# A gated-attention kernel: where VectorE makes the low half of the next tile's normalized rows

## The chip, the cores and the metric

One core of one Trainium2 chip runs the whole kernel. The metric is the device time of one execution in microseconds (us), lower is better; what is compared is the median of several runs. The engines are TensorE (PE in the profile), VectorE (DVE), ScalarE (ACT), GpSimd (POOL) and SyncE (SP, which only issues DMAs here). Each runs its own instruction stream in order; they meet only at semaphores.

## The reference

Two sandwiched blocks work on x of shape (2, 4096, 512) in float32. The first is linear attention over 16 heads, the second a gated linear attention (GLA) with a dense path and four sparse "expert" paths, chosen by a router.

```python
x = x + layernorm(attn(layernorm(x)))
x = x + layernorm(ffn(layernorm(x)))

# attn: q, k = relu(x@Wq), relu(x@Wk);  z = 1/(sum_n(k).q + eps);  out = (v k^T) q * z @ w_proj.T + b
# ffn (xn = layernorm(x)), 8 heads of 64, chunks of 64 rows:
q1, k1, v = xn@Wq*scale, xn@Wk, xn@Wv
q2, k2   = xn@Wqa@Wqb*scale, softmax(xn@Wka@Wkb)
gk1, gk2 = log_sigmoid(xn@Wg1a@Wg1b+bg1)/16, log_sigmoid(xn@Wg2a@Wg2b+bg2)/16
e = softmax(xn@We);  mask = one_hot(argmax(e));  rw = e*mask
o = gla(q1, k1, v, gk1) + sum_e gla(q2*rw_e, k2*rw_e, v, gk2*mask_e)
o = o * rsqrt(mean(o*o)+eps) * norm_w * silu(xn@Wga@Wgb)
return o @ Wo
# gla, chunk by chunk: scores of gated q and k under a causal mask, plus q times the carried state S;
# S <- S*decay + k_out^T v
```

## The kernel before

The rows are cut into 64 tiles of 128 rows (32 for each batch element). A first pass over all tiles normalizes x, makes keys and queries of the attention, writes the queries to DRAM and sums the moments that give the attention's context. The second pass, which takes three quarters of the time, goes over the tiles once more, one **step** for each tile n, and does everything else. A matrix in full precision is kept as a pair of float16 matrices, a high and a low part, and TensorE multiplies with three matmuls (`mm3`: high by high, high by low, low by high). The normalized rows of the second block are such a pair: `xn[:, 0]` and `xn[:, 1]`.

Everything is written out by hand: each engine has its own `step` function, and loops (`Fori`) that hold two steps each. A step is software-pipelined over several tiles. Step n does

- **ahead** for tile n+2: the attention's denominator (`den`), `ahead_qz` and its split into high and low (`ahead_qz_split`), the product with the mixing matrix (`y_mm`), its norm, and the first residual `x1`; ScalarE then makes rstd and the high part of xn (`ahead_norm2`, which increments `xnh_ok`), and VectorE the low part (`ahead_low`, which increments `xn_ok`);
- **front** for tile n: projections, router, gates, gated q and k, scores, state products;
- **back** for tile n-1: carry of the state (`back_carry1`, `back_carry`), masks, the select of the router's expert among the products with the state (`back_select`), the join, and the output's norm;
- **tail** for tile n-2: the output projection and the last residual (`back_out`).

SyncE's queue turns xn of tile n+1 into its transpose xnT with one DMA (`turn_xn`, L238). It waits for `q1_pe`, the last use of the old xnT by TensorE, and then for `xn_ok`. Behind it in the same queue stand the store of an output tile, the loads of two tiles and the transpose of og. TensorE reads the new xnT at the end of step n, in `route(n + 1)` and `low_rank(n + 1)`.

Lines that matter below. On VectorE: L1172 is `ahead_low`; L1198 and L1207 are the carry (the carry waits for `u_pe`, TensorE's state products L470, and for GpSimd's state); L1242 is the first instruction of `front_router`, which waits for the router's matmuls and for `low1_ok`, the third of ScalarE's copies of the low rows (L729 to L731); L1178 and L1186 are the masks of the scores; L1254 and L1257 are `front_onehot`; L1217 and L1220 are the select; L1277 is `front_logsig`; L1161 is the second half of the split of qz; L1314, L1315 and L1321 are the gated products; L1349 is `back_out`; L1168 is the residual x1. On GpSimd: L1044 adds the two masked scores (`back_am`), L1060 multiplies k2 with its gate (`front_k2`); in the first pass L1039 adds keys. On TensorE: L367 is the first matmul of `project_k2`, which waits for the select; L490 the products of q2 with the state, which the select reads; L443 the transposes of gated q and k. On ScalarE: L678 is a square with a row sum, L710 the high part of xn, L716 a residual's copy that waits for `back_out`, L747 the last of three instructions on the gates.

In one step of the state two instructions of the carry are memsets instead of sums: step 32, where the second batch element begins. In the last two steps with a front nothing is done ahead.

Of the kernel before, what the change touches and what calls it, by code (L numbers as in the profile page):

```python
# [10 lines left out]
ALL = BATCH * TILES  # L11
# [35 lines left out]
def sandwich_kernel(nc, x_d, wqkv_d, wproj_d, bproj_d, wb_d, wl_d, ws_d, wo_d, nw_d, consts_d, out_d):  # L47
# [11 lines left out]
    with ExitStack() as ctx:  # L59
# [122 lines left out]
        def S(name):  # L182
            if name not in sems:
                sems[name] = ctx.enter_context(nc.semaphore(name))
            return sems[name]
# [20 lines left out]
        def cur(n):  # L206
            return n + 2

        def prev(n):
            return n + 1  # L210
# [917 lines left out]
        def _(dve):  # L1128
# [29 lines left out]
            def split(n, dst, src, high, done):  # L1158
                ve.tensor_copy(dst[:, 0], src).then_inc(S(high), 1)
                dve.wait_ge(S(high), n + 1)  # L1160
                ve.tensor_tensor(dst[:, 1], src, dst[:, 0], ALU.subtract).then_inc(S(done), 1)  # L1161
# [8 lines left out]
            def ahead_low(n, p):  # L1170
                dve.wait_ge(S("xnh_ok"), cur(n))
                ve.scalar_tensor_tensor(xn[:, 1], x1[:, p, :], rstd[:, 1, :], xn[:, 0], ALU.mult, ALU.subtract).then_inc(S("xn_ok"), 1)  # L1172

            def back_masks(n):
                dve.wait_ge(S("a_pe"), n * 2 + 2)
                dve.wait_ge(S("o_pe"), prev(n))
                for odd in range(2):
                    last = ve.tensor_tensor(am1[:, odd, :, :], bank[(2, 5)[odd]].rearrange("p (a b) -> p a b", a=PAIRS),  # L1178
                                            causal.unsqueeze(1).to_broadcast([P, PAIRS, P]), ALU.mult)
                last.then_inc(S("am1_ok"), 1)  # L1180
# [9 lines left out]
            def back_carry1(n, reset):  # L1190
                dve.wait_ge(S("u_pe"), cur(n))
                dve.wait_ge(S("state_ok"), cur(n))
                if reset:
                    ve.memset(carry0, 0.0).then_inc(S("carry1_ok"), 1)
                    return
                for odd in range(2):
                    h = slice(odd * D2, odd * D2 + D2)
                    last = ve.tensor_tensor(carry0[h, :, h], bank[1][h, 0:PAIRS * D2].rearrange("p (a b) -> p a b", a=PAIRS),  # L1198
                                            state0[h, :, h], ALU.add)
                last.then_inc(S("carry1_ok"), 1)  # L1200

            def back_carry(n, reset):
                if reset:
                    ve.memset(carryx, 0.0).then_inc(S("carry_ok"), 1)
                    return
                for half in range(2):
                    last = ve.tensor_tensor(carryx[:, 2 * half:2 * half + 2, :], bank[3 * half].rearrange("p (r c) -> p r c", r=2),  # L1207
                                            statex[:, 2 * half:2 * half + 2, :], ALU.add)
                last.then_inc(S("carry_ok"), 1)
# [28 lines left out]
            def front_router(n):  # L1238
                dve.wait_ge(S("route_pe"), cur(n))
                dve.wait_ge(S("low1_ok"), cur(n))  # L1240
                logits = bank[7][:, 2 * P:2 * P + NEXP]
                ve.reduce_max(lmax[:, :], logits, X).then_inc(S("lmax_ok"), 1)  # L1242
                dve.wait_ge(S("lmax_ok"), n + 1)
                ve.scalar_tensor_tensor(lscore[:, :], logits, lmax[:, :], score, ALU.is_equal, ALU.mult).then_inc(S("lscore_ok"), 1)
                ve.tensor_scalar(ldiff[:, :], logits, lmax[:, :], None, ALU.subtract).then_inc(S("ldiff_ok"), 1)

            def front_label(n):
                dve.wait_ge(S("lscore_ok"), n + 1)
                ve.reduce_max(lab[:, :], lscore[:, :], X).then_inc(S("lab_ok"), 1)
# [9 lines left out]
            def front_prob(n):  # L1259
                dve.wait_ge(S("lexp_ok"), cur(n))  # L1260
                ve.reciprocal(rr[:, :], lsum[:, :]).then_inc(S("rr_ok"), 1)
                dve.wait_ge(S("rr_ok"), n + 1)
                ve.tensor_scalar(rq[:, :], rr[:, :], D2 ** -0.5, None, ALU.mult).then_inc(S("rq_ok"), 1)
# [72 lines left out]
            def ahead_qz_split(n):  # L1336
                dve.wait_ge(S("qzf_ok"), n + 1)
                dve.wait_ge(S("y_pe"), prev(n))
                split(n, qz16.rearrange("p x a b -> p x (a b)"), qz[:, :], "qzh_ok", "qz_ok")
# [8 lines left out]
                dve.wait_ge(S("x1m_ok"), cur(n))  # L1348
                ve.scalar_tensor_tensor(ob[:, p, :], bank[7], rstd[:, 2, :], xr[:, p, :], ALU.mult, ALU.add).then_inc(S("out_ok"), 1)  # L1349

            def step(n, p, b, front=True, back=True, tail=True, ahead=True, reset=False):
                m, mp, t = n - 1, 1 - p, n - 2
                if back:
                    back_carry1(m, reset)
                    back_carry(m, reset)
                if front:
                    front_router(n)
                    front_label(n)
                if back:
                    back_masks(m)  # L1360
                    back_masks2(m)
                if front:
                    front_masks(n)
                    front_low(n)
                    front_onehot(n, p)
                if back:
                    back_select(m, mp)
                if front:
                    front_prob(n)
                if back:  # L1370
                    back_join(m)
                if front:
                    front_kmax(n)
                    front_kdiff(n)
                    front_logsig(n)
                if back:
                    back_norm(m)
                if front:
                    front_ksum(n)
                    front_lslow(n)  # L1380
                    front_kfac(n)
                    front_sil(n, p, tail)
                if ahead:
                    ahead_qz(n + 2, p, b)
                    ahead_qz_split(n + 2)
                if front:
                    front_gated_1(n)
                    front_gated_q2(n)
                if tail:
                    back_out(t, p)  # L1390
                if front:
                    front_decay(n, p)
                if ahead:
                    ahead_residual(n + 2, p)
                    ahead_low(n + 2, p)

            def tile_stats(g, t):
                u = g * GT + t
# [87 lines left out]
            ahead_low(0, 0)  # L1486
            ahead_residual(1, 1, at=5, again=False)
            ahead_low(1, 1)
            step(0, 0, 0, back=False, tail=False)
            step(1, 1, 0, tail=False)  # L1490
            with dve.Fori(2, TILES - 2, 2) as n:
                step(n, 0, 0)
# [6 lines left out]
                step(n, 0, 1)  # L1499
                step(n + 1, 1, 1)  # L1500
            step(ALL - 2, 0, 1, ahead=False)
            step(ALL - 1, 1, 1, ahead=False)
            step(ALL, 0, 1, front=False, ahead=False)
            step(ALL + 1, 1, 1, front=False, back=False, ahead=False)


def layouts(i):
# [65 lines left out]
```

## Time and profile before

| | |
|---|---|
| median of 3 runs | 2510.76 us (2510.54 to 2510.84) |
| the profiled execution, its time | 2513.41 us |
| its span in the profile | 2511.6 us |
| granted TensorE clock, mean | 0.993 of full |
| TensorE busy | 2401.4 us, 96% |
| VectorE busy | 1782.2 us, 71% |
| ScalarE busy | 1561.9 us, 62% |
| GpSimd busy | 1136.7 us, 45% |

The span is from the first to the last instruction of the profiled execution; "busy" counts an engine's instructions alone. A busy share of 96% says that TensorE has little idle time, and not which wait makes it; that has to be read from a step of the second pass. In a timeline the columns are: start in us, duration in us, engine, line and operation, output and inputs, count, and in square brackets the engine's idle time before it with what ended that. An instruction that is held by something that is no semaphore shows a longer duration, and no idle time. Instructions of one engine overlap by some hundredths, so one may start before the end of the last.

### The profile page before, as it was taken

How to read it: one execution, taken by the hardware profiler on the slowest of the kernel's cores; microseconds unless marked ns; L12 is line 12 of the kernel's file. 1: busy time of each engine (PE TensorE's matmuls, PEld its weight loads, DVE VectorE, ACT ScalarE, POOL GpSimd, SP SyncE). 2: the span in 40 equal slices, each digit the busy share in tenths (PEclk: the TensorE clock that was granted, in tenths of full speed). 3: DMA queues.
4: the chain of work that ended last, by engine and by line, in shares of the span. 5: the costliest groups of instructions: out<-in, count | busy, mean ns of one | idle time of the engine just before them, and what ended most of it. 6: DMA issues, size and time to landing. Idle time of an engine off the chain costs nothing.

```text
span 2511.6 us, 56360 instructions
## 1 busy us (share of the span) xinstructions
PE 2401.4 (96%) x20208; PEld 1431.2 (57%) x20208; DVE 1782.2 (71%) x3484; ACT 1561.9 (62%) x3281; POOL 1136.7 (45%) x929
## 2 busy tenths in 40 slices
PE   4999999997999999999999999999999999999997
PEld 1444444454666666666666666666666666666664
DVE  4444444426778888888777888888887788888875
ACT  2322332226777777777777777777777777777773
POOL 1797333313444444444444444444444444444444
PEclk9999999998999999999999999999999999999998
DMA  6434433311111111111111111111111111111111
GB/s 218 101 100 134 101 101 100 86 53 34 47 44 48 42 46 42 42 42 42 43 48 44 47 44 45 42 42 42 42 46 46 50 42 46 42 42 42 42 26 35
DMA packets 250704, 145.65 MB, mean 58 GB/s; under 512 B 208096, under 2 KB 208096, under 8 KB 250144
## 3 DMA queue, kind: packets, MB, share of 16 engines
q1 hardware_dynamic: 240048, 119.32, 19.1%
q10 hardware_dynamic: 9504, 17.31, 1.8%
q0 software_dynamic: 1104, 8.40, 0.9%
q8 instruction: 28, 0.46, 0.1%
q14 instruction: 20, 0.16, 0.0%
HBM read 61.09 MB, written 33.55 MB: 38 GB/s over the span
## 4 chain that ended last, share of the span: by engine, by line
PE 55%; DVE 24%; ACT 9%; issue 8%; POOL 3%; SPq 1%; DMA 1%; DVEq 0%; ACTq 0%; POOLq 0%
PE psum L319 13%; PE psum L321 13%; PE psum L320 13%; PE psum L586 6%; DVE region L1220 6%; DVE region L1186 3%; ACT junk L678 3%; DVE region L1207 2%; PE psum L331 2%; DVE region L1178 2%; DVE region L1217 2%; ACT region L710 2%; DVE region L1198 2%; ACT region L686 2%; PE psum L367 2%
## 5 line engine op out<-in xcount | busy, mean ns | idle before, releaser
L319 PE MATMUL psum<-wb,region 128*128 128x512 f16 x768 | 293.7, 382 | 0.0
L320 PE MATMUL psum<-wb,region 128*128 128x512 f16 x768 | 292.5, 381 | 0.0
L321 PE MATMUL psum<-wb,region 128*128 128x512 f16 x768 | 292.3, 381 | 0.0
L1056 POOL TENSOR_TENSOR region<-region,kfac 128x512 f32<-128x512 f32 x64 | 66.7, 1042 | 447.2 <-DVE kfac L1309 447.2
L1039 POOL TENSOR_TENSOR region<-region 128x1024 f32<-128x1024 f32 x64 | 147.8, 2309 | 265.9 <-DVE region L1414 233.9
L1414 DVE SCALAR_TENSOR_TENSOR region<-psum,region 128x512 f16<-128x512 f32 x64 | 44.3, 692 | 225.2 <-ACT region L868 225.2
L1044 POOL TENSOR_TENSOR region<-region 128x1024 f32<-128x1024 f32 x64 | 150.9, 2357 | 105.4 <-DVE region L1186 105.4
L1051 POOL TENSOR_SCALAR region<-region,m 128x512 f32<-128x512 f32 x256 | 172.6, 694 | 26.8 <-DVE hm L1257 26.8
L586 PE MATMUL psum<-region 128*128 128x512 f16 x768 | 176.2, 379 | 2.1 <-DVE region L1414 2.1
L1084 POOL TENSOR_TENSOR og<-og 128x512 f16<-128x512 f32 x64 | 74.2, 1160 | 190.8 <-ACT og L810 190.8
L1172 DVE SCALAR_TENSOR_TENSOR region<-region,rstd 128x512 f16<-128x512 f32 x64 | 48.1, 752 | 143.2 <-ACT region L710 143.2
L1220 DVE SCALAR_TENSOR_TENSOR region<-psum,m,region 128x512 f32<-128x512 f32 x192 | 144.2, 751 | 6.8
L1168 DVE SCALAR_TENSOR_TENSOR region<-psum,rstd,region 128x512 f32<-128x512 f32 x64 | 48.1, 751 | 140.8 <-issue 138.1
L686 ACT ACTIVATE region<-psum 128x512 f32<-128x512 f32 x256 | 137.3, 589 | 0.0
L1410 DVE TENSOR_TENSOR region<-region 128x512 f16<-128x512 f32 x64 | 102.4, 1600 | 49.0 <-ACT region L881 49.0
L763 ACT ACTIVATE region<-psum 128x512 f32<-128x512 f32 x64 | 38.2, 597 | 156.9 <-PE psum L321 156.9
L1067 POOL TENSOR_TENSOR region<-region,decay 128x512 f32<-128x512 f32 x64 | 67.0, 1047 | 150.9 <-DVE decay L1326 150.9
L1060 POOL TENSOR_TENSOR region<-region 128x512 f32<-128x512 f32 x64 | 81.3, 1271 | 111.2 <-ACT region L777 111.2
L453 PE MATMUL psum<-region 64*128 64x128 f32 x2048 | 131.5, 278 | 0.0
L490 PE MATMUL psum<-region 64*128 64x256 f32 x1024 | 129.5, 393 | 2.0 <-DVE region L1178 2.0
L319 PE MATMUL psum<-wqk,region 128*128 128x512 f16 x256 | 97.7, 382 | 34.3 <-DMA region<-region 34.3
L586 PEld LDWEIGHTS psum<-region 128*128 128x128 f16 x768 | 74.9, 98 | 93.5 <-DVE region L1414 3.6
(232 smaller groups left out, 7252.4 us busy)
## 6 DMA issues: line engine op xcount, KB each, us to landing
region<-x_in SPq DMA_DIRECT2D x128, 256.0 KB, 2.6
q_cols<-region ACTq DMA_DIRECT2D x64, 256.0 KB, 2.5
region<-q_cols SPq DMA_DIRECT2D x64, 256.0 KB, 2.8
out_rows<-region SPq DMA_DIRECT2D x62, 256.0 KB, 2.0
region<-wb_in POOLq DMA_DIRECT2D x1, 3072.0 KB, 11.5
region<-wqkv_in SPq DMA_DIRECT2D x4, 512.0 KB, 6.1
region<-region SPq DMA_TRANSPOSE x128, 3.0
region<-ws_in POOLq DMA_DIRECT2D x1, 1280.0 KB, 15.6
```

Of the source, the lines that this page charges most:

```text
L319: mm(out, lhs(0), rhs(0), start=start, stop=False)
L320: mm(out, lhs(0), rhs(1), start=False, stop=False)
L321: return mm(out, lhs(1), rhs(0), start=False, stop=stop)
L453: last = mm(bank[where[odd]][:, pr * P:(pr + 1) * P], kT[h, pr, :], qT[h, pr, :], start=True, stop=True)
L490: last = mm(psum[:, 2 * half + odd, r * 256:r * 256 + 256], q2T[h, 2 * half + r, :], statex[h, 2 * half + r, :], start=True, stop=True)
L586: last = mm(bank[4 + j], xn8[:, p * GT + t, x * C + j * P:x * C + (j + 1) * P], k16[:, y_, :], start=first and begins, stop=final and ends ...
L686: ac(dst.rearrange("p a b -> p (a b)"), bank[where], ACT.Copy).then_inc(S(done), 1)
L1039: nc.gpsimd.tensor_tensor(kacc[b], kacc[b], k16, ALU.add).then_inc(S("kacc_ok"), 1)
L1044: nc.gpsimd.tensor_tensor(am1[:, :, :, :], am1[:, :, :, :], am2[:, :, :, :], ALU.add).then_inc(S("am_ok"), 1)
L1051: last = nc.gpsimd.tensor_scalar(vm[:, e, :], v[:, p, :], m4[:, p, e:e + 1], 1.0, ALU.mult, ALU.mult)
L1220: ve.scalar_tensor_tensor(to, of[:, :, e, :], m4[:, p, e:e + 1], to, ALU.mult, ALU.add).then_inc(S("sel_ok"), 1)
L1410: ve.tensor_tensor(xn8[:, p * GT + t, C:2 * C], xf, xn8[:, p * GT + t, 0:C], ALU.subtract).then_inc(S("xn8_ok"), 1)
```

## The change

In a step of the second pass, VectorE called `ahead_low(n + 2, p)` as its very last action. It now calls `ahead_low(n + 1, mp)` in the middle of the step, between `ahead_qz_split` and `front_gated_1`. A tile's low rows are thus made one step later than before. The prologue still makes those of tiles 0 and 1; step 0 makes none, steps 1 to 62 make those of tiles 2 to 63. Nothing else moves on any engine, and no instruction is added or taken away.

```diff
-            def step(n, p, b, front=True, back=True, tail=True, ahead=True, reset=False):
+            def step(n, p, b, front=True, back=True, tail=True, ahead=True, reset=False, late=True):
...
                 if ahead:
                     ahead_qz(n + 2, p, b)
                     ahead_qz_split(n + 2)
+                if late:
+                    ahead_low(n + 1, mp)
                 if front:
                     front_gated_1(n)
                     front_gated_q2(n)
...
                     front_decay(n, p)
                 if ahead:
                     ahead_residual(n + 2, p)
-                    ahead_low(n + 2, p)
...
-            step(0, 0, 0, back=False, tail=False)
+            step(0, 0, 0, back=False, tail=False, late=False)
...
             step(ALL - 2, 0, 1, ahead=False)
-            step(ALL - 1, 1, 1, ahead=False)
-            step(ALL, 0, 1, front=False, ahead=False)
-            step(ALL + 1, 1, 1, front=False, back=False, ahead=False)
+            step(ALL - 1, 1, 1, ahead=False, late=False)
+            step(ALL, 0, 1, front=False, ahead=False, late=False)
+            step(ALL + 1, 1, 1, front=False, back=False, ahead=False, late=False)
```

VectorE's instructions at the turn of a step in the loop, before (in brackets what each waits for; `xnh_ok` is ScalarE's high part of xn, `u_pe` TensorE's state products, `low1_ok` ScalarE's low rows):

```order
L1326 TENSOR_TENSOR decay<-exs 128x20 [waits state_ok,exs_ok]
L1168 SCALAR_TENSOR_TENSOR region<-psum,rstd,region 128x512 [waits xc_ok,rstd0,x1m_ok]
L1172 SCALAR_TENSOR_TENSOR region<-region,rstd 128x512 [waits xnh_ok]
L1198 TENSOR_TENSOR region<-psum,region 64x4x64 [waits state_ok,u_pe]
L1198 TENSOR_TENSOR region<-psum,region 64x4x64
L1207 TENSOR_TENSOR region<-psum,region 128x512 x2
L1242 TENSOR_REDUCE lmax<-psum 128x1 [waits low1_ok,route_pe]
```

In the changed kernel the residual L1168 and the carry L1198 are neighbours there; the rest is as it was. The middle of the step on VectorE, after the change (`qzh_ok` is VectorE's own high part of qz, `q1_pe` TensorE's projection of q1):

```order
L1159 CAST region<-region 128x512 [waits y_pe,qzf_ok]
L1161 TENSOR_TENSOR region<-region 128x512 [waits qzh_ok]
L1172 SCALAR_TENSOR_TENSOR region<-region,rstd 128x512 [waits xnh_ok]
L1314 SCALAR_TENSOR_TENSOR region<-psum,region 128x512 [waits q1_pe,e1_ok]
L1315 SCALAR_TENSOR_TENSOR region<-psum,region 128x512
```

Before, L1314 stood right behind L1161; now L1172 is between them, with no other semaphore than its own. The streams of TensorE, ScalarE, GpSimd and SyncE are the same in both kernels.

## Rows read from the trace of the kernel before

**Rows 1.** Windows from L367 to L367: length; busy PE, PEld, DVE, ACT, POOL; clock, DMA.

```profile
1154.14:1184.03 29.89, 29.20 (x279) 18.52 (x279) 23.99 (x50) 21.92 (x47) 13.71 (x12) 1.00 0.17 44
1482.66:1512.43 29.77, 29.20 (x278) 18.52 (x279) 23.90 (x50) 21.90 (x47) 13.72 (x12) 1.00 0.17 45
1512.43:1542.02 29.59, 29.20 (x278) 18.52 (x279) 23.37 (x48) 21.72 (x47) 13.69 (x12) 1.00 0.20 45
```

**Rows 2.** Waits of TensorE, 1000 to 2300 us: total, times, longest.

```profile
PE psum L367 <- DVE region L1220: 29.3, 44, 0.7
```

**Rows 3.** Timeline of all engines, turn of a step in the loop.

```profile
1170.10 1.90 PE L470 MATMUL psum<-region 128*64 128x256 f32 x16
...
1171.52 0.72 ACT L710 ACTIVATE region<-region,rstd 128x512 f16<-128x512 f32 x1
...
1172.28 0.75 DVE L1172 SCALAR_TENSOR_TENSOR region<-region,rstd 128x512 f16<-128x512 f32 x1 [2.25 <-ACT region L710]
...
1172.95 0.85 DVE L1198 TENSOR_TENSOR region<-psum,region 64x256 f32<-64x256 f32 x2
...
1173.78 0.38 ACT L729 ACTIVATE region<-psum 64x256 f16<-64x256 f32 x1 [0.57 <-PE psum L321]
...
1174.44 0.26 ACT L731 ACTIVATE region<-psum 64x128 f16<-64x128 f32 x1
```

**Rows 4.** Timeline of all engines, router to one-hot rows of the same step.

```profile
1175.04 0.15 DVE L1242 TENSOR_REDUCE lmax<-psum 128x1 f32<-128x4 f32 x1
...
1176.88 1.28 DVE L1186 TENSOR_TENSOR region<-psum,same_c 128x512 f32<-128x512 f32 x2
...
1178.24 2.36 POOL L1044 TENSOR_TENSOR region<-region 128x1024 f32<-128x1024 f32 x1 [1.58 <-DVE region L1186]
...
1178.41 2.00 PE L490 MATMUL psum<-region 64*128 64x256 f32 x16
...
1180.06 0.56 DVE L1254 TENSOR_SCALAR m<-cst,lab 128x4 f32<-128x4 f32 x1
```

**Rows 5.** Timeline, the same step behind the select.

```profile
1184.46 1.49 ACT L747 ACTIVATE region<-region 128x1536 f32<-128x1536 f32 x1
...
1186.10 1.75 DVE L1277 SCALAR_TENSOR_TENSOR region<-psum,region 128x1536 f32<-128x1536 f32 x1
```

**Rows 6.** Timeline, last step with a front; none moved ahead of it.

```profile
2456.09 0.26 ACT L731 ACTIVATE region<-psum 64x128 f16<-64x128 f32 x1
...
2456.45 0.16 DVE L1242 TENSOR_REDUCE lmax<-psum 128x1 f32<-128x4 f32 x1 [0.28 <-ACT region L731]
...
2458.19 1.28 DVE L1186 TENSOR_TENSOR region<-psum,same_c 128x512 f32<-128x512 f32 x2
```

**Rows 7.** Timeline of all engines, split of qz to the next norm, loop step.

```profile
1192.69 0.69 DVE L1161 TENSOR_TENSOR region<-region 128x512 f16<-128x512 f32 x1
...
1193.45 1.26 POOL L1060 TENSOR_TENSOR region<-region 128x512 f32<-128x512 f32 x1 [1.75 <-ACT region L777]
...
1194.27 0.69 DVE L1314 SCALAR_TENSOR_TENSOR region<-psum,region 128x512 f32<-128x512 f32 x1 [0.89 <-PE psum L321]
1194.36 1.23 SPq L238 DMA_TRANSPOSE region<-region  x1
...
1196.91 0.72 ACT L716 ACTIVATE region<-region,xkeep 128x512 f32<-128x512 f32 x1 [1.70 <-DVE region L1349]
...
1197.63 1.91 PE L443 MATMUL psum<-cst,region 128*128 128x128 f32 x16
1197.83 0.60 ACT L678 ACTIVATE junk<-psum 128x512 f32<-128x512 f32 x1 [0.20 <-PE psum L321]
```

**Rows 8.** Landing times of L238's DMAs, whole kernel.

```profile
DMA to landing us min/median/max: 3.0/3.0/4.8
```

**Rows 9.** Timeline, first pass, VectorE and GpSimd side by side.

```profile
400.74 2.36 POOL L1039 TENSOR_TENSOR region<-region 128x1024 f32<-128x1024 f32 x1 [5.41 <-DVE region L1414]
...
401.88 1.77 DVE L1410 TENSOR_TENSOR region<-region 128x512 f16<-128x512 f32 x1 [0.77 <-ACT region L881]
```

## The prediction, made before the changed kernel ran

> **What bounds the kernel now.** I read the second pass, since the change touches nothing else. Cutting it at the starts of one TensorE instruction, the first matmul of `project_k2` (L367), gives one step per window [rows 1]. A step inside VectorE's loops lasts 29.89 us and TensorE is busy for 29.20 of it, so 0.69 us is all that a better order can win from a step. TensorE's waits name that remainder: L367 waits 29.3 us in 44 steps, 0.67 each, for VectorE's L1220, the last product of the select [rows 2]. So TensorE runs through from L367 to the end of `intra` and then stands until the select is done.
>
> Now follow VectorE back from L1220. At the turn of a step [rows 3] it waits until 1172.28 for ScalarE's L710, runs L1172 (`ahead_low`, 0.75), and starts the carry, L1198, at 1172.95. TensorE's L470, which the carry really needs, had ended at 1172.00. Behind the carry comes the router's L1242 at 1175.04, although ScalarE's L731, which it needs, ended at 1174.70: 0.34 late. From L1242 on VectorE is back to back until L1186 ends at 1178.16 [rows 4]. GpSimd's L1044 (`back_am`) starts 0.08 later and runs until 1180.60; the little L1254 (`front_onehot`) starts at 1180.06 but ends at 1180.62, right behind L1044. Its 0.56 us for four columns is a wait for GpSimd. Hot rows, select and L367 follow. So the chain per step is L1172, carry, router, masks, GpSimd's add, one-hot, select, L367, and the delay of 0.34 us passes through it whole.
>
> **The change, part by part.**
>
> *Taken from the turn of the step:* the wait for L710 and L1172 itself, which costs 0.67 us in line (1172.28 to 1172.95 [rows 3]). The carry may then start with `u_pe`. In the last step with a front, where the step ahead of it has no `ahead_low`, the same carry runs and the router starts at 2456.45, 0.10 behind L731's end, after 0.28 of idling [rows 6]. This is what the changed kernel should look like in every step. The floor is L731 (TensorE's low-rank products, then ScalarE), which the change does not move. So L1242 gains 0.34 - 0.10 = 0.24 us, and not 0.67.
>
> *How much of it arrives.* From L731's end to L1186's end it is 3.46 in the loop [rows 3, 4] and 3.12 in that last step [rows 6]; 0.10 of the difference is that L1242 to the end of L1186 takes 3.12 in the loop and 3.02 in the last step, which I leave aside: 0.24 again. A second sample in the trace: in the step that resets the state, the carry is two memsets (it comes between 1512.43 and 1542.02), and this step took 29.59 against 29.77 of its neighbour [rows 1]. TensorE's busy time is the same, 29.20. The gain was 0.18. I take 0.22 for a loop step, with 0.18 and 0.24 as bounds.
>
> *What could bind next on this chain.* L1254 must start before GpSimd is through. It starts 0.54 before GpSimd's end, so an add that ends 0.24 earlier still ends last. The select needs TensorE's L490, which ends at 1180.41, while L1254 ends at 1180.62 and the hot rows follow [rows 4]: 0.21 of room plus the hot rows, about enough.
>
> *Put in between the split of qz and the gated products:* 0.67 us where VectorE idles 0.89 before L1314, waiting for TensorE [rows 7]. That shrinks a little. L1277 (`front_logsig`) needs ScalarE's L747, which ended 0.15 before it [rows 5]; ScalarE hangs on TensorE's gates, ahead of L367, and does not move with the gain. With a latency of 0.04 (L710 to L1172 [rows 3]) only 0.11 of the gain passes L1277, so relative to L367 everything behind it on VectorE comes 0.11 later, and the idle time is 0.78. 0.67 fits, with 0.11 to spare, and costs nothing. If that cover were gone, ScalarE has 0.20 before L678 (the norm of the tile ahead) and 0.57 before L729 (the low rows): nothing is late on the chain before these are used up [rows 3, 7]. The last tile's `xnh_ok` that the moved instruction waits for is a step old: no wait.
>
> *What waits for it later:* SyncE's transpose L238 waits for `q1_pe`, and then for `xn_ok`, which used to be a step old. It was issued at 1194.36 [rows 7]; the new `xn_ok` comes at about 1192.69 + 0.11 + 0.61 + 0.75 = 1194.16. Behind it in SyncE's queue stand the store, the two loads and og's transpose. It lands in 3.0 us, 4.8 at most [rows 8], and the router's matmuls read it behind L470, one step after 1172.00, so at 1201.8: 7.4 us after the issue. Even a microsecond of delay is covered.
>
> *Sum.* VectorE's loops hold 56 steps; the first still belongs to the pipeline's filling. 55 x 0.22 = 12.1. Six steps more (two of the filling, three around the middle, the last but one) I take at 0.13, my choice between nothing and the reset step's 0.18 since the filling waits for other things: 0.8. The reset step and the last have their gain already. Together 12.9 us. The profiled execution took 2513.41 us with a span of 2511.6 and would come to 2500.5; the median of the runs, 2510.76, which is 2.65 below, to 2497.9.
>
> **Rivals.**
>
> *The shared access of VectorE and GpSimd.* In the first pass L1410, a tensor_tensor with both inputs in SBUF, takes 1.77 us where it starts beside GpSimd's L1039 and ends at 403.65, 0.55 behind L1039's end of 403.10 [rows 9]; L1161, of the same shape, takes 0.69 [rows 7]. So it stood until GpSimd was nearly through. L1172 too reads two SBUF tensors, and its new place is beside GpSimd's L1060 (k2 times its gate). Counted from L367's start at 1184.03, L1060 starts at 9.42. L1172 would start at 8.66 (L1161) + 0.11 + 0.61 = 9.38 (the next instruction starts 0.08 before the end of one of this size, as L1198 behind L1172), first by 0.04, with an uncertainty as large. If VectorE is first, L1060 is held until about 10.0 and its product comes at 11.3, while TensorE's transposes (L443) only start at 13.6 [rows 7]: free. If GpSimd is first, L1172 ends 0.61 behind L1060's end (10.68), at 11.29, and L1314 starts at 11.21 for 10.24, 0.97 late. L1349 hands this to L716; L716 then starts at 13.85, L678 at 14.48 for 13.80, 0.68 late. The 0.57 before L729 take most, and 0.11 reaches the low rows. The gain would be 0.11 in such a step: 55 x 0.11 + 0.8 = 6.9, so 2503.9; if it alternates from step to step (a smaller gain puts L1172 earlier again), 10 us and 2501. This rival I give 0.20.
>
> By the Trainium skill ("SBUF — State Buffer", Who interferes with whom) a VectorE instruction with two SBUF inputs and a GpSimd instruction that reads SBUF exclude each other, and the order of issue decides who stands. By that rule the move is not free in either order; the trace agrees for tensor_tensor with the 1.77 us of L1410, and shows no long overlap for the form that is moved.
>
> *Nothing is won.* Another wait takes the 0.22: the select finds L490 (0.21 of room) or the one-hot finds its rows, or TensorE's cumulate finds VectorE's low logs later by the 0.11. Against it stands the reset step, which kept 0.18 with all of these in place. A gain under 0.09 a step is within 5 us: 2506 to 2511. Chance 0.07.
>
> *Slower.* It needs one thing: L1172 stuck in its new place for longer than all covers. 0.97 late still leaves 0.11 won, so the break-even is L1314 late by 1.08, and 5 us are lost from 1.17 on; each 0.1 beyond costs 5.5 us. GpSimd's L1060 would have to hold it for 0.2 longer than its own 1.26 us allow, or start later than it does, and ScalarE's L777, on which L1060 waits, moves with TensorE. At 1.3 late: 2523. Chance 0.03.
>
> **The numbers.** Forecast (VectorE first, or the delay swallowed), 0.70: its own range is 55 x 0.18 + 0.5 = 10.4 to 55 x 0.24 + 1.0 = 14.2, so 2496.5 to 2500.4. Lock collision 0.20, nothing 0.07, slower 0.03. The range must leave out no more than 0.2: from 2495.5, a little under the upper bound of the gain, to 2505, past the collision in every step. A measurement of this kernel tells 0.2%, 5.0 us, from no change. Forecast and nearly all of the collision are beyond it: faster 0.90, same 0.07, slower 0.03.
>
> **What the profile after would show.** L1242 idles before it, released by L731, and starts 0.10 behind it; L1198 starts well under 0.95 behind L470's end; TensorE's wait before L367 falls from 0.67 to about 0.45; the step lasts 29.65 in the loops; L1172 has no wait; the idle time before L1314 is near 0.1. L1060 starting as before but lasting about 1.8 says VectorE was first; L1172 at nearly 2 us and L1314 a microsecond late says GpSimd was. I am wrong if the step keeps its 29.88 (then look at what L1254 or L1217 ends its wait on), or if ScalarE's L729 is no longer released by TensorE.

## The result, and the profile after

The changed kernel takes 2498.91 us (median of 5 runs, 2496.37 to 2500.06) against 2510.84 (5 runs, 2510.54 to 2512.97): a ratio of 0.9947, 95% interval 0.9936 to 0.9958 (the ratio is the one that belongs to the interval; the two medians divide to 0.9952). It is faster by 11.9 us between the medians, half a per cent; 2497.9 was forecast.

| | before | after |
|---|---|---|
| the profiled execution, its time | 2513.41 us | 2496.37 us |
| its span | 2511.6 us | 2494.6 us |
| granted TensorE clock, mean | 0.993 | 0.995 |
| first to last L1242 (63 steps) | 1881.36 us | 1867.98 us |
| a step in the loops, mean of 55 | 29.875 us | 29.645 us |

The profiled execution of after was the fastest of its five, so the spans differ by 17.0 us, more than the medians do. Of this the second pass made 13.4. The pass began 2.55 us earlier (first L1242 at 572.54 instead of 575.09) though nothing ahead of it was changed; the granted clock was 0.97 there between 500 and 560 us instead of 0.94. Another 1.1 us lies behind the last L1242. What the change is worth is best read from the pass.

The windows from L367 to L367 answer to [rows 1]; columns as there.

```profile
1117.49:1147.13 29.64, 29.20 (x278) 18.48 (x279) 25.15 (x50) 21.75 (x47) 13.68 (x12) 1.00 0.17 44
1147.13:1176.78 29.65, 29.20 (x278) 18.43 (x278) 25.15 (x50) 21.78 (x47) 13.70 (x12) 1.00 0.17 44
```

TensorE's busy time is unchanged, VectorE's is 1.16 more for the same 50 instructions: one of them has become longer, as is shown below. TensorE's wait in the same stretch as [rows 2]:

```profile
PE psum L367 <- DVE region L1220: 19.3, 43, 0.7
```

That is 0.45 us each time instead of 0.67. The turn of the step and the select, which answer to [rows 3, 4]:

```profile
1133.46 1.90 PE L470 MATMUL psum<-region 128*64 128x256 f32 x16
...
1135.41 0.86 DVE L1198 TENSOR_TENSOR region<-psum,region 64x256 f32<-64x256 f32 x2 [1.42 <-PE psum L470]
...
1137.80 0.26 ACT L731 ACTIVATE region<-psum 64x128 f16<-64x128 f32 x1
...
1138.16 0.16 DVE L1242 TENSOR_REDUCE lmax<-psum 128x1 f32<-128x4 f32 x1 [0.58 <-ACT region L731]
...
1141.36 2.35 POOL L1044 TENSOR_TENSOR region<-region 128x1024 f32<-128x1024 f32 x1 [1.34 <-DVE region L1186]
...
1141.78 2.00 PE L490 MATMUL psum<-region 64*128 64x256 f32 x16
...
1143.24 0.50 DVE L1254 TENSOR_SCALAR m<-cst,lab 128x4 f32<-128x4 f32 x1
...
1143.96 0.75 DVE L1217 TENSOR_SCALAR region<-psum,m 128x512 f32<-128x512 f32 x1
...
1147.13 0.39 PE L367 MATMUL psum<-ws,region 128*128 128x512 f16 x1 [0.43 <-DVE region L1220]
```

The carry starts 0.05 behind L470's end (0.95 before), and the router's L1242 stands idle and starts 0.10 behind L731's end (0.34 before). The middle of the next step, answering to [rows 7]:

```profile
1155.94 0.69 DVE L1161 TENSOR_TENSOR region<-region 128x512 f16<-128x512 f32 x1
...
1156.55 1.82 DVE L1172 SCALAR_TENSOR_TENSOR region<-region,rstd 128x512 f16<-128x512 f32 x1
1156.56 1.26 POOL L1060 TENSOR_TENSOR region<-region 128x512 f32<-128x512 f32 x1 [1.61 <-ACT region L777]
...
1158.30 0.68 DVE L1314 SCALAR_TENSOR_TENSOR region<-psum,region 128x512 f32<-128x512 f32 x1
...
1160.92 0.72 ACT L716 ACTIVATE region<-region,xkeep 128x512 f32<-128x512 f32 x1 [2.60 <-DVE region L1349]
...
1161.55 0.58 ACT L678 ACTIVATE junk<-psum 128x512 f32<-128x512 f32 x1
```

There is most of the 1.16: L1172 now lasts 1.82 where it took 0.75, with no idle time ahead of it, and ends beyond GpSimd's L1060, which starts 0.01 after it and keeps its 1.26. It stood until L1060 was nearly through. (The rest is overlap of neighbours, which busy time counts once: the durations by themselves add up to 1.03 more.) This is so for 56 of the 64 L1172; the durations of the two lines (ns, least, median, most) say it:

```profile
L1172 DVE SCALAR_TENSOR_TENSOR region<-region,rstd x64: 744/1832/1851, 565.2 to 2429.2; 128x512 f16<-128x512 f32 x64
L1060 POOL TENSOR_TENSOR region<-region x64: 1262/1269/1840, 589.7 to 2458.8; 128x512 f32<-128x512 f32 x64
```

What hangs on L1172 is late at first: L1314 starts 11.17 behind L367, L716 13.79 and L678 14.42, where it was 10.24, 12.88 and 13.80. ScalarE no longer idles before L678 and, in most steps, before L729; and L729 starts 0.107 behind the start of TensorE's L453 in both kernels (means over the loops). So L1172 became 1.07 us longer in the middle of the step, and of the 0.62 that were left of it at L678 nothing passed ScalarE's 0.57 us of idle time before L729. The little that is missing is overlap: where ScalarE does not idle, an instruction starts up to 0.1 before the recorded end of the last.

### The profile page after: what moved, and what is told of

It is laid out like the page before. It is cut to its first block and busy times, and to the rows that moved or that the text cites. A ratio compares the mean times of both kernels' runs of the same rounds, so it can differ in the third digit from the quotient of the medians.

```text
span 2494.6 us, 56360 instructions
## 1 busy us (share of the span) xinstructions
PE 2397.7 (96%) x20208; PEld 1424.4 (57%) x20208; DVE 1848.0 (74%) x3484; ACT 1554.0 (62%) x3281; POOL 1138.6 (46%) x929
## 5 line engine op out<-in xcount | busy, mean ns | idle before, releaser
L1039 POOL TENSOR_TENSOR region<-region 128x1024 f32<-128x1024 f32 x64 | 147.8, 2309 | 266.2 <-DVE region L1415 233.7
L1044 POOL TENSOR_TENSOR region<-region 128x1024 f32<-128x1024 f32 x64 | 150.5, 2352 | 92.3 <-DVE region L1186 92.3
L1067 POOL TENSOR_TENSOR region<-region,decay 128x512 f32<-128x512 f32 x64 | 67.1, 1048 | 199.0 <-DVE decay L1326 199.0
L716 ACT ACTIVATE region<-region,xkeep 128x512 f32<-128x512 f32 x64 | 46.3, 723 | 156.3 <-DVE region L1349 156.3
L1168 DVE SCALAR_TENSOR_TENSOR region<-psum,rstd,region 128x512 f32<-128x512 f32 x64 | 48.1, 751 | 123.4 <-issue 120.7
L1084 POOL TENSOR_TENSOR og<-og 128x512 f16<-128x512 f32 x64 | 74.1, 1158 | 139.7 <-ACT og L810 139.7
L453 PE MATMUL psum<-region 64*128 64x128 f32 x2048 | 131.5, 278 | 0.0
L1060 POOL TENSOR_TENSOR region<-region 128x512 f32<-128x512 f32 x64 | 83.7, 1307 | 104.0 <-ACT region L777 104.0
L490 PE MATMUL psum<-region 64*128 64x256 f32 x1024 | 127.9, 389 | 2.0 <-DVE region L1178 2.0
```

Source lines behind the costliest of these rows:

```text
L453: last = mm(bank[where[odd]][:, pr * P:(pr + 1) * P], kT[h, pr, :], qT[h, pr, :], start=True, stop=True)
L490: last = mm(psum[:, 2 * half + odd, r * 256:r * 256 + 256], q2T[h, 2 * half + r, :], statex[h, 2 * half + r, :], start=True, stop=True)
L1039: nc.gpsimd.tensor_tensor(kacc[b], kacc[b], k16, ALU.add).then_inc(S("kacc_ok"), 1)
L1044: nc.gpsimd.tensor_tensor(am1[:, :, :, :], am1[:, :, :, :], am2[:, :, :, :], ALU.add).then_inc(S("am_ok"), 1)
```

## Experiments

All kernels are edits of the changed kernel (called "after") unless it is said otherwise. The ratio is to runs of the kernel before that were taken beside them (medians 2510.65 to 2512.71). "Step" is the mean of the same 55 steps in VectorE's loops.

| run | edit | median us | ratio to before, 95% | step us |
|---|---|---|---|---|
| (after) | | 2498.91 | 0.9947, 0.9936 to 0.9958 | 29.645 |
| e1_behind_carry | L1172 behind the carry | 2499.16 | 0.9945, 0.9929 to 0.9962 | 29.650 |
| e9_ahead_of_split | L1172 ahead of the split | 2498.23 | 0.9946, 0.9929 to 0.9963 | 29.642 |
| e2_behind_gated | L1172 behind the gated products | 2497.44 | 0.9942, 0.9925 to 0.9959 | 29.644 |
| e2b_behind_decay | L1172 behind front_decay | 2502.77 | 0.9963, 0.9949 to 0.9977 | 29.644 |
| e3_twice | L1172 twice | 2525.20 | 1.0052, 1.0035 to 1.0068 | 30.02 |
| e4_after_onehot | one-hot ahead of the masks | 2551.95 | 1.0165, 1.0148 to 1.0182 | 30.50 |
| e8_gated_onehot | e2 and e4 | 2554.27 | 1.0170, 1.0153 to 1.0187 | 30.57 |
| e6_before_onehot | kernel before, one-hot as e4 | 2557.74 | 1.0185, 1.0168 to 1.0202 | 30.59 |
| e10_between_masks | one-hot between the masks | 2498.56 | 0.9946, 0.9930 to 0.9963 | 29.633 |
| e11_mask_alone | half of the one-hot there | 2497.33 | 0.9941, 0.9925 to 0.9958 | 29.630 |
| e12_select_halves | e10, select in halves | 2498.55 | 0.9948, 0.9935 to 0.9962 | 29.65 |
| e13_halves_alone | select in halves | 2507.61 | 0.9982, 0.9973 to 0.9991 | 29.79 |

### Where did the gain come from: L1172 behind the carry

```diff
                     back_carry(m, reset)
+                if late:
+                    ahead_low(n + 1, mp)
                 if front:
                     front_router(n)
...
-                if late:
-                    ahead_low(n + 1, mp)
```

> VectorE makes the low rows of tile n+1 at the turn of step n, but behind the carry and ahead of the router. The same work stands ahead of the router as in the kernel before; only its wait for ScalarE no longer stands ahead of the carry. Theory A (the router's floor is ScalarE's third copy of the low rows, and the wait ahead of the carry was what mattered): the carry starts right behind TensorE's L470, the 0.57 us that VectorE idles before the router in the changed kernel take the 0.67 us of the moved instruction, the router starts at most 0.1 later behind ScalarE's copy than in the changed kernel; a loop step of 29.65 to 29.75 us, 2499 to 2505 us. Theory B (the 0.67 us of work ahead of the router was what mattered): the router stays about 0.3 behind the copy, a step of 29.85 us, 2509 to 2511 us. No collision with GpSimd's L1060 in either; VectorE's L1314 is released by TensorE again.

```profile
1167.99 0.86 DVE L1198 TENSOR_TENSOR region<-psum,region 64x256 f32<-64x256 f32 x2 [2.01 <-PE psum L470]
...
1170.09 0.74 DVE L1172 SCALAR_TENSOR_TENSOR region<-region,rstd 128x512 f16<-128x512 f32 x1
...
1170.39 0.26 ACT L731 ACTIVATE region<-psum 64x128 f16<-64x128 f32 x1
...
1170.75 0.16 DVE L1242 TENSOR_REDUCE lmax<-psum 128x1 f32<-128x4 f32 x1
```

The step is 29.650, as short as the changed kernel's, with L1172 still between the carry's start and the router. Its 0.74 fill the idle time for L731, and L1242 starts as early behind L731 as in after, 0.10. So theory A held. The numbers add up: in the kernel before, the carry stood 0.90 later than it had to behind L470 (0.95 instead of 0.05), 0.67 of it L1172's work and 0.23 the wait for L710 [rows 3]. VectorE's 0.58 of idle time before L1242 and the 0.08 by which neighbours overlap cover the work. What cost 0.23 a step was thus the wait that came on top. The work by itself is free here because this cover is as long as the work, and not in general.

### Does the collision cost: three other places

```diff
 e9:            ahead_qz(n + 2, p, b)
+               ahead_low(n + 1, mp)
                ahead_qz_split(n + 2)
 e2:            front_gated_q2(n)
+               ahead_low(n + 1, mp)
                back_out(t, p)
 e2b:           front_decay(n, p)
+               ahead_low(n + 1, mp)
                ahead_residual(n + 2, p)
```

> The changed kernel with the moved instruction one place earlier, between ahead_qz and its split. Theory A (order of issue decides who stands; now the split's L1161 meets L1060 and TensorE's y_mm waits for it): L1161 is held until L1060 is nearly over, 1.8 us, qz comes about 0.5 us later than TensorE wants it, step up to 30.1 us, 2510 to 2526 us, or less if VectorE wins the race in every other step. Rival (the place among VectorE's instructions is of no account, since 0.1 to 0.8 us are idle there): 29.65 us, 2497 to 2500 us.

> The moved instruction stands behind the three gated products and ahead of back_out, where GpSimd's L1060 is over. Theory A (the collision of the changed kernel is swallowed by ScalarE's idle time and costs nothing): the instruction takes 0.75 us again instead of 1.83, L1314 starts 10.2 us behind L367 instead of 11.2, and the step stays at 29.65 us, 2497 to 2500 us. Rival (the collision reaches the low rows by up to 0.11 us a step): the step falls to 29.55 to 29.6 us, 2493 to 2496 us.

> The moved instruction stands behind front_decay and ahead of the residual, where VectorE waits some 2 us anyway: it uses no cover at all, but SyncE's transpose can only be issued some 14.2 us behind L367, 3.4 us before TensorE's router matmuls want its result. Theory A: with a landing time of 3.0 us nobody waits, step 29.65 us, 2497 to 2500 us. Rival (the late transpose becomes the wait): TensorE idles before the router's matmuls, each 0.1 us of it lengthens a step by 0.1; at the 4.8 us of the slowest landing seen a step of 31 us and 2580 us.

In e2 no L1172 of the 64 lasts over 0.752 us: there is no collision, and the step is 29.644 against 29.645. The collision costs nothing, as theory A had it. In e9 it is L1161, a tensor_tensor with two SBUF inputs, that meets GpSimd, first by 0.08:

```profile
1217.06 0.69 DVE L1161 TENSOR_TENSOR region<-region 128x512 f16<-128x512 f32 x1
1217.14 1.74 POOL L1060 TENSOR_TENSOR region<-region 128x512 f32<-128x512 f32 x1 [1.61 <-ACT region L777]
1217.96 0.69 DVE L1314 SCALAR_TENSOR_TENSOR region<-psum,region 128x512 f32<-128x512 f32 x1 [0.21 <-PE psum L321]
```

VectorE wins, GpSimd lasts 1.74, and L1314 has 0.21 of idle time again. Theory A, by which that place costs up to 0.45 a step, fell: 29.642, the rival's value. In e2b the loops are as fast, but the last step with a front takes 28.60 instead of 27.45 and one in the middle 30.17 instead of 29.63. (In e2 they are 27.86 and 29.74, and after has 27.45 and 29.63.) The median, 2502.77, lies beyond the 2497 to 2500 of theory A, which holds for the loops alone; these two steps add 1.7 us to after's time. The transpose of xn, which waits for L1172, is too late for TensorE in a step that is shorter than the others:

```profile
2437.48 0.75 DVE L1172 SCALAR_TENSOR_TENSOR region<-region,rstd 128x512 f16<-128x512 f32 x1
...
2438.31 1.23 SPq L238 DMA_TRANSPOSE region<-region  x1
...
2441.40 0.18 PE L319 MATMUL psum<-wl,region 128*128 128x4 f16 x1 [1.09 <-DMA region<-region]
```

The place is not free of a meeting with GpSimd either: L1172 starts 0.16 ahead of L1067 (the state's decay), keeps its 0.75, and L1067 takes 1.49 (median) instead of 1.05. The loops show no cost of it.

### How much can VectorE carry there: L1172 twice

```diff
+        spare = sb("spare", 2, C, dt=f16)
...
             def ahead_low(n, p):
                 dve.wait_ge(S("xnh_ok"), cur(n))
+                ve.scalar_tensor_tensor(spare[:, p, :], x1[:, p, :], rstd[:, 1, :], xn[:, 0], ALU.mult, ALU.subtract)
```

The kernel does the work once more into a tensor that nobody reads.

> The changed kernel with the moved instruction issued twice in its new place, the first time into a spare tensor. Theory A (the delay of 1 us by the collision has used up ScalarE's idle time before its low rows exactly, so any further delay reaches the router): L729 comes 0.4 to 0.65 us later, the step is 30.05 to 30.3 us, 2523 to 2538 us. Rival (there is more cover left than ScalarE's idle time shows): 29.65 to 29.75 us, 2497 to 2505 us.

```profile
1198.40 0.75 DVE L1173 SCALAR_TENSOR_TENSOR spare<-region,rstd 128x512 f16<-128x512 f32 x1
1198.55 1.73 POOL L1061 TENSOR_TENSOR region<-region 128x512 f32<-128x512 f32 x1 [1.75 <-ACT region L778]
1199.07 1.76 DVE L1174 SCALAR_TENSOR_TENSOR region<-region,rstd 128x512 f16<-128x512 f32 x1
```

The line numbers are one or two higher here. The first takes the access and GpSimd is held, then the second is held by GpSimd. Counted from L490, the second ends about 0.62 later than L1172 does in after. The step grows by 0.375 us (30.02, just under theory A's least of 30.05), so some 0.25 of cover were left in after. The way is not only the expected one over ScalarE's low rows. Before L367 TensorE waits 0.58 a step instead of 0.45; and the second half of its state products (L470, here L471), which waits for the residual L1168 (here L1169), is held by it, as it never is in after: its weight loads stand for 0.47 us. By TensorE's starts in three steps, some 0.15 of the delay stand at L367 and 0.2 at L470.

```profile
1205.33 0.75 DVE L1169 SCALAR_TENSOR_TENSOR region<-psum,rstd,region 128x512 f32<-128x512 f32 x1 [1.89 <-issue]
...
1206.13 0.63 PEld L471 LDWEIGHTS psum<-region 128*64 128x64 f32 x8 [0.47 <-DVE region L1169]
```

### Is L1254's wait for GpSimd the next thing to win: the one-hot ahead of the masks

```diff
                     front_label(n)
+                    front_onehot(n, p)
                 if back:
                     back_masks(m)
...
                     front_low(n)
-                    front_onehot(n, p)
```

> The changed kernel, with the one-hot rows (L1254, L1257) made right behind the router's label instead of behind the low rows, so that GpSimd's add L1044 cannot hold them. Theory A (L1254's 0.50 us is GpSimd's hold, and the next floor is TensorE's L490): L1254 takes 0.2 us or less, the select starts 0.1 to 0.15 behind L490's end, which is 0.04 to 0.08 earlier than now; step 29.56 to 29.61 us, 2493 to 2497 us. Rival (L1254 is long for a reason of its own, 0.5 us wherever it stands): the masks come 0.5 later, the step is 29.65 us or longer, 2499 us or more.

> Both orders together: the moved instruction behind the gated products (no collision with L1060) and the one-hot rows behind the label. Theory A (L490 is the floor of both): the step is that of the one-hot change alone, 29.56 to 29.61 us, and not the sum of the two gains; 2492 to 2496 us. Rival (the gains add): 29.88 - 0.23 - 0.31 = 29.34 us, 2479 us.

> The kernel before, with only the one-hot rows moved up behind the router's label; ahead_low stays at the end of the step. Theory A (the chain per step is wait, L1172, carry, router, masks, GpSimd's add, L1254, select; the change wins because the select's next floor, L490's end, lies 0.3 us ahead): L1254 falls from 0.56 to 0.2 us or less, the select starts right behind L490's end, the step falls from 29.88 to about 29.57 us, 2492 to 2496 us: as much as the change and a little more, with the wait ahead of the carry untouched. Rival (the turn of the step is what counts, the one-hot rows are beside the chain): step 29.88 us, 2510 to 2512 us.

e4 and e8 are slower than after by 0.9 us a step, and e6 is slower than before by 0.7. All three theories fell. Of the rivals, that of e4 has only its direction ("or longer") right: L1254 is not long for a reason of its own, since it takes 0.23 in 20 of e4's 64 steps. Those of e8 and e6 (29.34 and 29.88) fell too. The little instructions were only moved from one GpSimd instruction to another (run e4):

```profile
1213.91 1.19 POOL L1084 TENSOR_TENSOR og<-og 128x512 f16<-128x512 f32 x1 [2.17 <-ACT og L810]
1214.13 1.00 DVE L1257 TENSOR_TENSOR hm<-m,cst 128x8 f16<-128x8 f32 x1
...
1216.83 1.14 PE L490 MATMUL psum<-region 64*128 64x256 f32 x8
...
1218.19 1.13 PE L490 MATMUL psum<-region 64*128 64x256 f32 x8 [0.22 <-DVE same_c L1271]
```

The masks come later, and with them L1271, for which the second half of TensorE's L490 waits, and the low rows L1236, for which the gates wait. In this step L1236 ends at 1219.40, and the first matmul of the gates (L366) starts at 1219.46. In e6 the same happens with L1254, held 1.00, and L490 waits 0.48.

### The same without that collision

```diff
                     back_masks(m)
+                    front_onehot(n, p)
                     back_masks2(m)
```

In the second kernel only L1254 is put there, and L1257 stays.

> The changed kernel with the one-hot (L1254 and L1257) moved forward to between the two masks, where GpSimd is idle: L1084 has just ended, and L1044 waits for the second mask. Theory F (the hold of L1254 was nearly free, since TensorE's L490 ends only about 0.2 us before the select starts, and L490 itself waits for the last reader of the label's row, L1271): L1254 and L1257 last 0.23 and 0.17, but the second mask and L1271 end 0.39 later, L490 starts and ends 0.39 later, the select starts 0.35 to 0.4 later than in the changed kernel, and the loop step is 29.95 to 30.05 us instead of 29.65: the median 2515 to 2522, slower than before. Theory G (the hold is what bounds the select and L490 has room for it): the 0.3 us of hold are won, the step is 29.35 to 29.6, the median 2482 to 2496.

> The changed kernel with only the first half of the one-hot (L1254, which the select needs) moved to between the two masks; the second half (L1257, which only GpSimd needs) stays in front of the select and is held there in its place until GpSimd's L1044 is nearly through. Theory F: 0.15 to 0.2 us are put ahead of L490, nothing is won behind it: the loop step is 29.70 to 29.85, the median 2502 to 2510, L490 starts 0.15 to 0.2 later, the select 0.1 to 0.2 later. Theory G (L1044's end rules, L490 has room): only L1257 is left behind it, the step is 29.40 to 29.60 and the median 2487 to 2496.

Both theories fell in both runs: the steps are 29.633 and 29.630, as in after. Run e10:

```profile
1142.01 0.22 DVE L1254 TENSOR_SCALAR m<-cst,lab 128x4 f32<-128x4 f32 x1
...
1143.79 2.00 PE L490 MATMUL psum<-region 64*128 64x256 f32 x16
...
1143.89 0.34 DVE L1271 SCALAR_TENSOR_TENSOR same_c<-psum,lab,cst 128x128 f32<-128x128 f32 x1
...
1145.94 0.75 DVE L1217 TENSOR_SCALAR region<-psum,m 128x512 f32<-128x512 f32 x1 [0.35 <-PE psum L490]
...
1149.11 0.39 PE L367 MATMUL psum<-ws,region 128*128 128x512 f16 x1 [0.40 <-DVE region L1220]
```

The hold is gone (0.22), VectorE is free 0.35 early, and then waits for L490, which was not delayed: only its second eight matmuls need L1271, and they had about half a microsecond of room. The select starts 0.15 behind the end of L490; after had 0.18 and before 0.45. So with the change L490 came within 0.03 of being the limit of the select, and that is all that the hold of L1254 is worth.

### What holds the step now: the select in halves

The bank halves that L490's first eight matmuls write are read before the others; eight instructions of 256 columns alternate between the halves.

```diff
-                dve.wait_ge(S("ix_pe"), cur(n))
+                dve.wait_ge(S("ix1_pe"), cur(n))
...
+                for e in range(NEXP):
+                    for part, h in enumerate((slice(H2 // 2, H2), slice(0, H2 // 2))):
+                        if e == 0:
+                            if part:
+                                dve.wait_ge(S("ix_pe"), cur(n))
+                            ve.tensor_scalar(to[:, h], of[:, h, 0, :], m4[:, p, 0:1], None, ALU.mult).then_inc(S("sel_ok"), 1)
```

> The kernel with the one-hot between the masks, and the select cut in two halves of 256 columns: the half that reads the banks of L490's first eight matmuls starts at once, the other when L490 has ended, and the eight instructions alternate between the halves. Theory H (in the changed kernel the end of L490, then the select, is what holds L367: TensorE idles 0.40 us there and nowhere else): VectorE's idle time of 0.35 before the select is used, and the step falls by what the select ends earlier. An instruction of 256 columns takes between 0.34 us (what 512 columns take in a row, 0.60, less half of 512 columns' own time) and 0.43 (the carry's 64x256) from start to start: seven behind L490's end make 2.4 to 3.0 us where four of full width made 3.0, so the step falls by up to 0.4 us, from 29.63 to 29.25 to 29.63; my value is 29.40, the median about 2484 (2474 to 2499). Rival J (something further up, L731 or TensorE's own queue ahead of L490, sets the step): the select ends earlier but the step stays at 29.6.

> The changed kernel with the select in halves as in the run above, but with the one-hot where it was, held behind GpSimd's L1044. VectorE has no idle time before the select, so all eight instructions come behind the start of today's four: 8 x 0.34 to 0.43 is 2.7 to 3.4 us against 3.0. Theory H: the step is 29.35 (0.3 less) to 30.0, my value 29.60, and at least 0.1 longer than in the run with the one-hot moved: there the hold of the one-hot, worth nothing with the undivided select, begins to cost. Rival J: both kernels have the same step.

An instruction of a half takes about 0.40 from start to start, so eight make 3.28 from the first start to L367 where four made 3.17. In e12 the select ends 0.2 earlier all the same, and TensorE's wait before L367 falls from 0.40 to 0.20; but the step does not fall:

```profile
1143.90 2.00 PE L490 MATMUL psum<-region 64*128 64x256 f32 x16
...
1149.02 0.39 PE L367 MATMUL psum<-ws,region 128*128 128x512 f16 x1 [0.20 <-DVE region L1225]
...
1149.94 1.48 ACT L747 ACTIVATE region<-region 128x1536 f32<-128x1536 f32 x1
...
1151.46 1.76 DVE L1282 SCALAR_TENSOR_TENSOR region<-psum,region 128x1536 f32<-128x1536 f32 x1 [0.28 <-ACT region L747]
...
1154.34 1.23 DVE L1293 SCALAR_TENSOR_TENSOR region<-region 128x1024 f16<-128x1024 f32 x1
...
1155.77 0.38 PE L424 MATMUL psum<-region,centred 128*128 128x512 f16 x1
```

What was won before L367 is lost before L424, the cumulated logs (L1282 and L1293 are the L1277 and L1288 of the other kernels). They hang on a second chain that never passes the select: TensorE's gates behind L490, ScalarE's three instructions up to L747, VectorE's L1277, ScalarE's L755, VectorE's L1288, then L424, 0.20 behind its end. The idle time for L747 before L1282 is 0.28 here. My theory H, that TensorE waits "nowhere else", fell; rival J has the step right, but not its reason, which lies beside the select and not further up. The distance from L490's start to L424's start shows it, read from each timeline, with the step at that place; the rest is their difference:

| kernel | L490 to L424 | step there | rest |
|---|---|---|---|
| before | 12.13 | 29.89 | 17.76 |
| after | 11.87 | 29.64 | 17.77 |
| e10 | 11.88 | 29.63 | 17.75 |
| e12 | 11.87 | 29.63 | 17.76 |
| e13 | 11.99 | 29.76 | 17.77 |
| e4 | 12.57 | 30.32 | 17.75 |
| e6 | 12.82 | 30.59 | 17.77 |

From L424 on to the next L490 TensorE takes the same 17.76 us in all of them, and the whole difference lies between L490 and L424. There the gates' chain allows 11.87 (L1288 ends 11.67 behind L490 in after), and in after the select's chain gives the same: L367 at 5.35, then 6.52 of matmuls. In e13 the select alone is slower by 0.11, and the step by 0.12 in the first batch element: that chain binds at once again. In the second batch element the steps are longer in both, 29.83 instead of 29.76 in e13 and 29.66 instead of 29.63 in e12; what makes them so stays open. None of these kernels is shown to be faster than after.

## Why the prediction was right, by its steps

- **The floor is L731, and L1242 gains 0.24.** Right: 0.10 behind L731's end, as forecast from the last step; L1198 0.05 behind L470; L1172 without a wait.
- **0.22 of it arrive.** It was 0.23, the wait before L367 is 0.45 as forecast, and the step 29.645 for 29.65. I took the value from two samples and did not see how near the next limits were. "0.21 of room plus the hot rows, about enough" was nearly used up (0.18 behind L490's end, where 0.15 is the least), and the path L1277 to TensorE's cumulate, which I named under "nothing is won" only, sets 11.87 where before had 12.11 (mean; 12.13 in the table's step): at most 0.24 to 0.26 was to be had. The forecast kept below both limits without having priced the second, which is luck; e10 to e12 show that nothing beyond 0.015 was left.
- **VectorE is first, by 0.04, and 0.67 us fit into its idle time.** Wrong. It starts 9.42 behind L367, GpSimd 9.43, and GpSimd gets the access; L1172 takes 1.82 us, and the 0.89 of idle time before L1314 do not hold that. I had 9.38 and 9.42. VectorE is later than I had it because L1277 comes 0.14 later behind L367 (2.21 for 2.07), and not 0.11. I called the uncertainty as large as the difference; that was so, but 0.70 against 0.20 was no fair split of a draw (part of the 0.70 stood for the delay being swallowed).
- **The collision's price, 0.11 a step.** Its chain came as worked out: L1314 at 11.17 (11.21 forecast), L716 at 13.79 (13.85), L678 at 14.42 (14.48). Each is 0.04 to 0.06 earlier, since L1172 ends 0.55 behind L1060 and not 0.61, and the last 0.05 was swallowed on ScalarE by the overlap that I had left out at L729, which starts 0.107 behind L453's start in both kernels. The price is nothing that can be measured (29.645 against e2's 29.644). This is why the total is the forecast's though the mechanism is the rival's: the forecast was written for either way, but that the delay is swallowed was not worked out, and its coming true is luck. The page "SBUF — State Buffer" of the Trainium skill (Who interferes with whom), which says that such a pair excludes each other, is borne out by the 1.82 us; that the move is then "not free in either order", as the prediction put it, is not: what a collision costs was decided by the cover behind it.
- **SyncE's transpose.** Covered in the loops, as forecast. e2b shows where it would not be, with a later place for L1172: in the short last step with a front, and once in the middle, at 1.2 and 0.5 us.
- **Sum.** 55 x 0.23 is 12.7, the pass as a whole 13.4, so 0.7 is left beside the loops. It looks like the 0.8 that I took for six other steps, but is not: 0.67 of it is the first interval from L1242 to L1242 alone (30.90 before, 30.23 after), which lasts anything from 29.93 to 33.60 in the kernels of this document; the seven others together gain 0.03. (Among them the last interval is 0.23 longer, because only its end stood at the floor in the kernel before.) So no run shows the term of 0.8. 12.9 were forecast and 11.9 measured between the medians; medians of the same kernel differ by up to two microseconds from one set of runs to another.

## What to carry to other kernels

An instruction with a late wait, placed ahead of one whose inputs are ready, delays it by wait and work together, and costs what the idle time further on does not cover; here that cover was just the work, and the wait was the cost. Look for the pair in which a releaser's end and the next start lie far apart, and move the waiting one to where the engine idles. Before counting on more than that, measure every chain between two fixed points of the busiest engine's own stream; here two of them lay within 0.02 us of each other, and three further improvements of one (e10, e11, e12) were worth nothing that can be measured. Where two instructions may collide, price the collision to the end of its chain for either winner; if both end in idle time, who wins does not matter to the time.

## What the runs showed of the hardware

- Engines meet not only at semaphores. GpSimd's L1060 holds a scalar_tensor_tensor of VectorE with two SBUF inputs, 1.82 us instead of 0.75 (after), as L1039 held the tensor_tensor L1410 in the first pass. The other way round L1060 is itself held, 1.71 to 1.84 instead of 1.26, where VectorE is less than 0.17 ahead (after, e3, e9); in e2b L1067 takes 1.49 instead of 1.05.
- Who gets the access is not who starts first in the records. In the meetings of L1172 (e3: its first copy) or L1161 with L1060 in all kernels of this document, GpSimd won all 299 in which the records put VectorE between 0.13 behind it and 0.034 ahead, and VectorE all 193 in which it was 0.035 or more ahead (in after at 1423.33, 1719.99 and 2075.72, by 0.037).
- Small instructions are held too: L1254 (128x4, SBUF alone) takes 0.22 to 0.23 when GpSimd is still (e10), 0.40 to 0.56 at the end of L1044 (before, after), and 1.00 to 1.23 beside L1084 (e6, e4); L1257 (128x8) takes 0.17, and 1.00 beside L1084 (e4).
